# The first projection of batches 1 to 3 moved into the first attention, in quarter tiles

## The reference

```
qkv = x @ qkv_w.T                         # q, k, v: 16 heads x 16
raw = q . k                               # per head, 2048 x 2048
scores  = sips_alpha * tanh(raw / sips_beta)
scores += lam * (tanh(x @ hex_w.T) . tanh(x @ hex_w.T)) / 2
scores += (hexc . Mh . hexc) / 6 * 2*sigmoid(scale_logit)   # hexc = tanh(x @ q6_w.T), Mh per head
scores  = where(causal, scores, -inf)
out     = softmax(scores) @ v             # then @ out_w.T
```

## Time and profile before

| | us |
|---|---|
| median of three runs | 4131.27 |
| profiled execution | 4128.27 |
| its span on the core | 4125.7 |
| PE busy in the span | 3703.2 (90%) |
| ACT busy | 3478.9 (84%) |
| DVE busy | 2592.8 (63%) |
| POOL busy | 425.9 (10%) |

### The profile page before, as it was taken

How to read it: one execution, slowest core, us unless ns; L and a number is a source line. 1 busy time by engine, 2 the same in 40 slices (tenths; PEclk the granted TensorE clock), 3 DMA queues, 4 the chain that set the end, 5 groups by cost and what they waited for, 6 DMA issues and landing times. The chain is left out here.

```text
span 4125.7 us, 61470 instructions
## 1 busy us (share of the span) xinstructions
PE 3703.2 (90%) x21943; PEld 1418.7 (34%) x21958; DVE 2592.8 (63%) x4548; ACT 3478.9 (84%) x2950; POOL 425.9 (10%) x407
## 2 busy tenths in 40 slices
PE   6978989989999989999889699969999999999787
PEld 2432323223323223323223366622222222222565
DVE  5647888788887788887788476633232323232688
ACT  2429999999999999999999566659999999999233
POOL 3540000000000000000000055510000000000232
PEclk9989999999999999999999899979999999999899
DMA  5862121111121111111121377632222222121331
GB/s 163 263 205 66 46 61 46 40 54 58 50 61 43 40 57 56 52 58 43 38 62 33 101 187 198 159 101 76 76 71 71 79 62 82 59 82 40 117 93 47
DMA packets 272882, 339.63 MB, mean 82 GB/s; under 512 B 39054, under 2 KB 206062, under 8 KB 272305
## 3 DMA queue, kind: packets, MB, share of 16 engines
q1 hardware_dynamic: 272564, 335.58, 27.7%
HBM read 207.18 MB, written 128.25 MB: 81 GB/s over the span
## 5 line engine op out<-in xcount | busy, mean ns | idle before, releaser
L842 DVE SCALAR_TENSOR_TENSOR att_prob<-att_tanh,alpha,ps 128x512 f32<-128x512 f32 x2176 | 1506.5, 740 | 410.3 <-ACT att_tanh L786 366.6
L726 PE MATMUL ps<-att_q,att_k 99*128 99x512 bf16 (+5 forms) x5120 | 1134.3, 350 | 114.8 <-DMA att_v<-v_ones 57.3
L755 PE MATMUL ps<-att_prob,att_v 128*32 128x512 f32 (+3 forms) x10240 | 1162.2, 540 | 2.0 <-ACT att_prob L795 1.9
L786 ACT ACTIVATE att_tanh<-ps,rbeta 128x2048 f32<-128x2048 f32 x544 | 1125.7, 2069 | 36.0 <-PE ps L726 36.0
L795 ACT ACTIVATE att_prob<-att_prob 128x2048 f32<-128x2048 f32 x544 | 1095.7, 2014 | 1.5 <-DVE att_prob L842 1.3
L792 ACT ACTIVATE att_prob<-ps 128x1024 f32<-128x1024 f32 x1088 | 1054.4, 1021 | 25.5 <-PE ps L726 9.5
L736 PE MATMUL ps<-att_f,att_g 75*128 75x512 bf16 (+3 forms) x2560 | 810.4, 354 | 133.4 <-DVE att_prob L842 121.6
L726 PEld LDWEIGHTS ps<-att_q,att_k 96*128 96x128 bf16 (+1 forms) x5120 | 399.2, 98 | 962.4 <-ACT att_prob L792 427.0
L831 DVE TENSOR_TENSOR att_prob<-att_prob,keep 128x512 f32<-128x512 f32 (+1 forms) x320 | 187.4, 586 | 580.2 <-ACT att_prob L792 579.2
L736 PEld LDWEIGHTS ps<-att_f,att_g 75*128 75x128 bf16 x2560 | 231.7, 96 | 927.9 <-DVE att_prob L842 906.9
L755 PEld LDWEIGHTS ps<-att_prob,att_v 128*32 128x32 f32 x10240 | 216.2, 108 | 347.7 <-ACT att_prob L792 142.0
(11 more groups left out here) (143 smaller groups left out, 2690.2 us busy)
## 6 DMA issues: line engine op xcount, KB each, us to landing
att_v<-v_ones SPq DMA_DIRECT2D x128, 256.0 KB
att_k<-k_parts SPq DMA_DIRECT2D x128, 192.0 KB
att_q<-q_parts SPq DMA_DIRECT2D x128, 192.0 KB
v_ones<-proj_vs SPq DMA_DIRECT2D x64, 256.0 KB, 3.8
att_k<-k_parts SPq DMA_DIRECT2D x128, 128.0 KB
att_q<-q_parts SPq DMA_DIRECT2D x128, 128.0 KB
o_t<-att_on SPq DMA_DIRECT2D x512, 32.0 KB, 1.7
v_ones<-mid_vs SPq DMA_DIRECT2D x64, 256.0 KB, 3.3
```

Of the source, the lines that this page charges most:

```text
L726: mm = pe.matmul(ps[:, bank, col:col + w], keys, q_s[:, n % QU, h, q0:q0 + w], start=True, stop=True)
L755: mm = pe.matmul(ps[VW * h:VW * (h + 1), O0 + n % 2, q0:q0 + w], v_s[:, c % KU, kb % CB, h * VW:(h + 1) * VW], prob[:, S % R, h, col:col + ...
L786: th.done(act.activation(tanh_s[:, S % 2], ps[:, QK0:QK0 + HQ], ACT.Tanh, scale=kn["rbeta"][:, 0:1]))
L842: sc.done(dve.scalar_tensor_tensor(prob[:, S % R, h], tanh_s[:, S % 2, h], kn["alpha"][:, 0:1], ps[:, E0 + h % 2], ALU.mult, ALU.add))
```

## The change

`project_phase` now does batch 0 only. The other 12 groups (X = 0 to 11) run inside the first attention, group X during set X, in nine units: `g`, `q` 0, `q` 1, `k` 0, `k` 1, `f` 0, `f` 1, `v` 0, `v` 1. A unit uses the output bank that is free at that time (bank 7 for `q` 0, `q` 1 and `k` 0, else bank 6). Its matmuls are cut into pieces of 256 columns and half of the contraction (`g`: two pieces of 512 columns; `f`: two pieces of 256), and `plan` gives each piece a step and a place. Place "a" is on PE between `extra` of head 1 and the next step's `scores`; place "b" is between `extra` of heads 2 and 3. When a unit's last piece stands at a step's place "a", DVE copies its bank out in the same step, ahead of that step's first sum. `g` is taken out by ACT with a tanh between tanh and exp. POOL does all four steps of the three-way split. SP stores the units, and loads inputs for group X+2; the row-max phase, skipped with these inputs, has a projection of its own.

```diff
-def project_phase(nc, kn, layer, w, x_d):
+def project_phase(nc, kn, layer, w, x_d, NB=B):
...
+    plan = ["9a 9b", "12a 12b 12b 13a", "13b 14a 14b 15a", "15b 16a 16b 19a", "24a 24b 24b 25a", "25b 26a", "26b 27a", "27b 28a 28b 29a", "29b 30a 30b 31a"]
...
+    bank_of = {u: O0 + (1 if 1 <= u <= 3 else 0) for u in range(NU)}
+    behind = {0: 0, 1: 1, 4: 2}
+    ahead = {2: 0, 3: 3, 0: 8}
...
+            def project(j, i, done):
+                X, kind, m, tile, n, bank = unit(j)
+                if i == 0:
...
+                    bg_ev.wait(pe, j - 1)
+                    if j % NU in behind:
+                        o_tr.wait(pe, X * GB + behind[j % NU])
...
+                else:
+                    lhs = (wq_s if kind == "q" else wk_s)[:, c, m * P:(m + 1) * P]
+                    mm = pe.matmul(ps[0:n, bank, cols], lhs, xt_s[:, X % 2, c, cols], start=c == 0, stop=c == DC - 1)
+                if done:
+                    bg_ps.done(mm)
...
                     extra(S, 0)
                     extra(S, 1)
+                    pieces_at(S, "a")
                     if S + 1 < N:
                         scores(S + 1, 0)
...
                     extra(S, 2)
+                    pieces_at(S, "b")
                     extra(S, 3)
...
+            def evict(j):
+                X, kind, m, tile, n, bank = unit(j)
+                if kind == "v":
+                    bg_ps.wait(dve, j)
+                    v_out.wait(dve, m, X - 1)
+                    bg_ev.done(dve.tensor_copy(vs[:, m, :, :, 0:HD], ps[:, bank].rearrange("p (t h d) -> p t h d", t=2, h=H)))
+                elif kind != "g":
+                    bg_ps.wait(dve, j)
+                    low.wait(dve, tile - 2)
+                    bg_ev.done(dve.tensor_copy(raw[0:n, tile % 2], ps[0:n, bank]))
...
                 pv.wait(dve, S - R)
                 for h in range(HQ):
+                    if h == 0 and unit_at(S) is not None:
+                        evict(unit_at(S))
                     if h == 2:
                         normalise(due, 1)
...
+                if S > 0 and unit_at(S - 1) is not None:
+                    feature(unit_at(S - 1))
...
+                for j in range(NX * NU):
...
+                    hi.done(pool.tensor_copy(parts[0:n, u, 0], src))
...
+                    rest.done(pool.tensor_tensor(rem[0:n], src, parts[0:n, u, 0], ALU.subtract))
...
+                    mid.done(pool.tensor_copy(parts[0:n, u, 1], rem[0:n]))
...
+                    low.done(pool.tensor_tensor(parts[0:n, u, 2], rem[0:n], parts[0:n, u, 1], ALU.subtract))
```

More of the change, by code:

```diff
@@ L655, in attend_phase @@
         on_s = ph.sb("on", [P, 2, TG])
+        if layer == 0:
+            w_in, x_in, ones_set = ph.sem("w_in"), [ph.sem(f"x_in{u}") for u in range(2)], ph.sem("ones_set")
+            bg_ps, bg_ev = ph.count("bg_ps"), ph.count("bg_ev")
+            hi, rest, mid, low = (ph.count(n) for n in ("hi", "rest", "mid", "low"))
+            parts_out, v_out = ph.stores("parts_out", 2), ph.stores("v_out", 2, NHQ)
+            wq_s, wk_s, wv_s = (ph.sb(n, [P, DC, D]) for n in ("wq", "wk", "wv"))
+            w12_s = ph.sb("w12", [P, DC, NF])
+            xt_s = ph.sb("xt", [P, 2, DC, TG])
+            f12 = ph.sb("f12", [NF, 2, TG])
+            raw = ph.sb("raw", [P, 2, TG])
+            rem = ph.sb("rem", [P, TG])
+            parts = ph.sb("parts", [P, 2, 3, TG], BF16)
+            vs = ph.sb("vs", [P, 2, 2, H, VW])
         ps = kn["ps"]
@@ L753, in weigh @@
                         o_tr.wait(pe, n - 2)
+                        X = it - 1 if g == 0 else it
+                        if g in ahead and 0 <= X < NX:
+                            bg_ev.wait(pe, X * NU + ahead[g])
                     for h in range(HQ):
@@ L779, in _, with feature @@
                 c.start(act)
+            def feature(j):
+                X, kind, m, tile, n, bank = unit(j)
+                if kind == "g":
+                    bg_ps.wait(act, j)
+                    if X >= 2:
+                        low.wait(act, tile - 2 * NTL)
+                    bg_ev.done(act.activation(f12[:, X % 2], ps[0:NF, bank], ACT.Tanh))
             for S in range(N + 1):
@@ L798, in _ @@
         def _(dve):
[L799 removed]
+            for c in (sc, o_tr, o_rc, o_mul, o_n, kept) + ((bg_ev,) if layer == 0 else ()):
                 c.start(dve)
@@ L856, in _, with row_max_phase @@
             assert not due
-def row_max_phase(nc, kn, layer):
+        if layer == 0:
+            @block.gpsimd
+            def _(pool):
+                for c in (hi, rest, mid, low):
+                    c.start(pool)
+                for j in range(NX * NU):
+                    X, kind, m, tile, n, bank = unit(j)
+                    if kind == "v":
+                        continue
+                    u = tile % 2
+                    src = f12[:, X % 2] if kind == "g" else raw[0:n, u]
+                    bg_ev.wait(pool, j)
+                    parts_out.wait(pool, u, tile // 2 - 1)
+                    hi.done(pool.tensor_copy(parts[0:n, u, 0], src))
+                    hi.wait(pool, tile)
+                    low.wait(pool, tile - 1)
+                    rest.done(pool.tensor_tensor(rem[0:n], src, parts[0:n, u, 0], ALU.subtract))
+                    rest.wait(pool, tile)
+                    mid.done(pool.tensor_copy(parts[0:n, u, 1], rem[0:n]))
+                    mid.wait(pool, tile)
+                    low.done(pool.tensor_tensor(parts[0:n, u, 2], rem[0:n], parts[0:n, u, 1], ALU.subtract))
+def row_max_phase(nc, kn, layer, w=None):
     SR, FR = QROWS, FROWS
@@ L935, in _ @@
                 if layer == 0:
+                    with act.Fori(0, B - 1) as b:
+                        for gq in range(GB):
+                            act.wait_ge(tile_ps, b * NTB + gq * NTL + 1)
+                            act.activation(f12[:], ps[0:NF, 3], ACT.Tanh).then_inc(feat, 1)
                     with act.Fori(0, B * NHQ) as it:
```

180 lines of the change are left out of this document (163 added, 17 removed).

## The result

The changed kernel takes a median of 4116.2 us (4112.9 to 4121.4, six runs) against 4129.8 for the kernel before on the same chips: 0.9967 of the time, interval 0.9953 to 0.9981. (Of six runs of the kernel before, one took 5905.5 us, a slow run, and is left out; the other five took 4128.4 to 4133.8.) It is faster by 0.3%. The forecast was 4051 and the range ended at 4103, so the direction was right and 65 us of the gain did not come.

The account below looks back on a forecast made before the run. PE was taken to bound the projection and ACT the first attention. 4128.3 - 172.9 removed + 89.4 for twelve groups + 3.0 at the start = 4047.8 us profiled, median 4051; eight in ten from 4000 to 4103.

Parts of the forecast that it names:

- The 172.9 us that go: Projection: twelve groups leave it at 14.41 us each, 172.9 us removed; batch 0 stays.
- Start, +3: Start of the first attention: six DMAs issued ahead of group 1's operands make PE wait, +3 us (0 to 7).
- Copy 0.62 from start to start: First attention, DVE: each PSUM-to-SBUF copy takes 0.62 us, after some 1.1 us idle waiting for a PE piece.
- the ring 0.7: Copies or pieces in neighbouring attention steps close a loop of waits through PE and DVE: 4.38 against 3.66, 0.7 us a step.
- The first rival: First attention: PE runs ahead, no loop of waits closes, copies cost little; 3.9 us a group, 4008 us; chance 0.23.
- the third: Attention pieces: weight loads exposed on PE, 0.38 us more a piece, 18.1 a group, slower at 4178 us; chance 0.03.
- The fourth: Batch borders: a later batch's loads wait for its projection's stores in SP's queue, 3 us each at three, 4060; chance 0.01.
- L818 reads two SBUF tensors while POOL works: Normalising product on DVE, steps 13 and 25: slowed 0.19 each by POOL, 0.4 us a group; at most 2.4.
- The granted clock is 1.00 ... in both: Projection and first attention: clock read at the 2.4 GHz level before the change; no cost entered for a fall.
- One sign named ahead: First attention: ACT idle before the tanh, released by the scores, would mean PE sets the price and the forecast is wrong.
- Small terms: First attention, per group: steps behind a copy 0.4, 29 and 31 1.1, `g` 0.5, 19 0.25.
- The second rival: First attention: PE over its room and L818 waiting for whole POOL operations, 11.3 us a group, 4097 us; chance 0.18.

Follow-up runs that it names:

- E3: Changed kernel with the last piece of units q1, f0, f1, v0, v1 moved to place b of the step before, copies unmoved; 4074.9 us.
- E4: Changed kernel with the `f` matmuls reading weights and inputs of 128 rows instead of 12, same columns; 4084.4 us, one run.
- E2: Changed kernel with POOL's four operations of a tile on 8 of 512 columns, all waits and stores kept; 4065.7 us, one run.
- E5: Changed kernel with a new plan: every unit behind `g` ends at place b, copy opens the next step, none at steps 13 and 25; 3978.4 us.
- E7: E5 with the normalising piece ahead of the copy and six DMAs of weights and inputs behind the third load instead of the first; 3986.0 us.

## Why the prediction was off

- **The 172.9 us that go: right.** The attention's first matmul is at 131.64 instead of 303.66; that is 172.0.
- **Start, +3: right.** The first three exps stand 13.8 us apart instead of 10.9 before. The wait is the one named:

```profile
144.92 1.89 PE L854 MATMUL ps<-att_q,att_k 96*128 96x512 bf16 x4 [4.54 <-DMA att_v<-v_ones]
```

  It was 1.81.
- **Copy 0.62 from start to start, its wait 1.1, the ring 0.7: right.** The copy is 0.69 long and the sum follows after 0.61; its wait is 1.20; steps 15, 29 and 31 lost 0.67 and 0.72, and E3 showed the ring by opening it. The piece is a little cheaper than the 0.50: the scores follow it after 0.44 (474.16 to 474.60). The first rival (no ring) is out. Weight loads cost nothing that shows, so the third is out too. The fourth did not occur: between 140 and 1760 us PE waited for a DMA once, at the start. POOL's chain is 3.5 us (0.61 + 1.15 + 0.61 + 1.15) and not 4.7, and no copy waited for it.
- **"L818 reads two SBUF tensors while POOL works ... the difference 0.19 at steps 13 and 25 is 0.4": this step failed.** I read the price from the mean of L1342, 877 against 690. That mean mixes two kinds, and a mean over instances most of which are not held is no price for one that always is. The source view of the kernel before (duration ns min/median/max) has it:

```profile
L1342 DVE TENSOR_TENSOR mid_rem<-mid_qcos,mid_parts x64: 655/683/1692, 2366.9 to 2707.1; 128x512 f32<-128x512 f32 x64
```

  Of its 64 instances the 21 that met a POOL `tensor_tensor` take 1012 to 1692, the other 43 at most 687. So a price of 0.3 to 1.0 for one that is held stood in the trace of before. In the changed kernel it was 0.94 twice a set: 21.6 us over 23 instances instead of 4.8 over twelve sets. The wait was thus known and its size was wrong: my bound of two POOL instructions, 2.4 a set, was near what came (1.9). The Trainium skill (SBUF — State Buffer, section "Who interferes with whom") says that a DVE instruction with two SBUF inputs contends with a GpSimd instruction that reads SBUF, and that issue order decides who blocks. I weighed that and set it aside, and the trace agrees with it: behind the subtraction the product takes 1.35, ahead of it 0.42 (set 8). The Trainium skill says there too that a DVE instruction with at most one SBUF input does not contend, outside of modes that use both port pairs; the copies, which read PSUM, kept their 0.69 in the seven cases in which they met a POOL instruction.
- **"The granted clock is 1.00 ... in both": true of before, and taken for after without a word: this step failed too.** The term was put at nothing, and no rival held a fall of the clock. It cost 26 us in the profiled execution, in six sets, at 3.9 to 6.1 each. E4 (128 rows), E2 (shorter stop) and E5 (hardly a stop) had none. One sign named ahead, ACT's idle in front of the tanh and released by the scores, did come, but its reading, that PE then sets the price, holds only in the falls.
- **Small terms, all too low:** steps behind a copy 0.81 instead of 0.4 (12 and 24, where PE has three pieces, were not among them), 29 and 31 1.44 instead of 1.1, `g` 0.76 instead of 0.5, 19 0.39 instead of 0.25, 26 and 27 2.18 instead of 2.05. Steps 13 and 25 without POOL's hold (E2) lose 1.20 each instead of 1.05.
- **The balance.** Forecast 4047.8 for the profiled execution. Per set 10.53 instead of 7.45, times 12: +37.0 (of it 21.4 steps 13 and 25 with the product, 4.28 instead of 2.5 a set; 15.6 the small terms); falls +26; removal 0.9 less, which adds 0.9; phases behind the first attention +2.5 (1827.7 us against 1825.2, and between 1823 and 1830 in the experiments; not explained). Sum 4114; it took 4112.9. The second rival gave 4097 for the right reason in part (L818 for whole POOL operations) and the wrong one in part (PE over its room: E5 does the same pieces at 1.6 a set).

**What stays open.** Why the clock falls in some sets and not in others with the same program, and why E3, with the same stop and `f` pieces in pairs, had it in more. E7 had two short falls behind a step that lost only 0.64, so the long stop is not needed in every case. What the 12 rows do is known from one execution (E4), whose `f` pieces read other weights and inputs as well.

## What to carry to other kernels

Work slipped into a full pipeline costs little by its length and much by its waits: before placing it, follow the loop from the instruction that waits for it back through the other engine, and put the producer half a step ahead of the consumer (E3: 2.9 us a set for nothing but that). Read a hold between two engines from the instances that meet, by the longest of a group, and not from its mean; then move the one that is held to where the other is silent (E5). And if the change brings a stop together with matmuls of few rows, allow for the clock.

## What the runs showed of the hardware

- A DVE `tensor_tensor` of 128x256 with two SBUF inputs goes from 0.42 to 1.35 us behind a POOL subtraction of 1.15 that began 0.08 earlier. Begun 0.21 ahead of the subtraction it is 0.42, and so it is with POOL's instructions on 8 columns (E2).
- A copy of 128x512 float32 from PSUM to SBUF on DVE is 0.69 us, also with POOL at work (seven cases); a transposition of 128x512 from SBUF to SBUF is 0.70, also with POOL at work (eleven cases). The copy delays the next sum by 0.61.
- POOL copies 128x512 float32 to bf16 in 0.61 us and subtracts in 1.16, and a tile of 12 rows takes as long (0.60 and 1.14).
- The granted clock fell to 0.50 (1.2 GHz) in six of twelve sets of the changed kernel, for some 17 us once (PE busy 15.94 of 16) and some 10 us five times, where the `f` matmuls had 12 rows; with 128 rows of the same columns it did not fall behind the start of the attention (E4, one execution).
